# A transformer of four layers: where the second bias of the feed-forward part is added

## The reference

```
mod = silu(c) @ w_ada + b_ada                    # 6 rows of 288 per sample: shift, scale, gate, twice
x = x + gate_1 * (attention(norm(x) modulated) @ wo + bo)
h = gelu((norm(x) modulated) @ w1 + b1)          # 1152 hidden channels
x = x + gate_2 * (h @ w2 + b2)
```

## Time and profile before

| | before |
|---|---|
| median of three runs | 2198.0 us (2194.46 to 2200.98) |
| profiled execution | 2202.24 us, span 2200.5 us |
| PE busy | 2004.8 us (91%), mean granted clock 0.946 |
| DVE busy | 1336.7 us (61%) |
| ACT busy | 1142.4 us (52%) |
| POOL busy | 208.3 us (9%), 311 instructions |

### The profile page before, as it was taken

The page is one execution under the profiler, slowest core; times in us unless marked ns, Lnnn a source line. Parts: engine busy times, 40 slices in busy tenths (PEclk is TensorE's granted clock), DMA queues, the critical chain, the costliest instruction groups (busy, mean ns, idle before and its releaser), DMA issues.

```text
span 2200.5 us, 38987 instructions
## 1 busy us (share of the span) xinstructions
PE 2004.8 (91%) x15592; PEld 1496.7 (68%) x15592; DVE 1336.7 (61%) x2940; ACT 1142.4 (52%) x1705; POOL 208.3 (9%) x311
## 2 busy tenths in 40 slices
PE   6988999899998999999899999989997898999998
PEld 4346578748974896698575566887886646474658
DVE  4747647656674677476658482463545858684842
ACT  2353734474656365545636556554344474747463
POOL 3000111111110110011110000001100000000001
PEclk9686999899989999999999999998899999999999
DMA  5234242343234232524331412446154141314101
GB/s 160 60 120 85 74 122 63 73 122 92 77 68 136 64 86 48 152 67 100 78 104 18 131 7 65 68 78 134 30 107 111 31 114 36 96 20 112 26 3 25
DMA packets 204731, 173.97 MB, mean 79 GB/s; under 512 B 54822, under 2 KB 164678, under 8 KB 204550
## 3 DMA queue, kind: packets, MB, share of 16 engines
q1 hardware_dynamic: 197974, 158.76, 31.0%
q0 software_dynamic: 6576, 12.71, 2.1%
HBM read 125.57 MB, written 40.11 MB: 75 GB/s over the span
## 4 chain that ended last, share of the span: by engine, by line
PE 61%; DVE 20%; ACT 11%; DMA 3%; issue 3%; SPq 2%; POOL 0%; ACTq 0%; POOLq 0%; DVEq 0%
PE PSA L1890 16%; PE PSA L1905 14%; DVE MX L1529 9%; PE PSA L1680 5%; PE PSA L1794 4%; PE PSA L1771 4%; PE PSA L1741 4%; ACT PB L1378 4%; PE PSA L1784 3%; PE PSA L1753 2%; DVE HH L1659 1%; PE PSA L1814 1%; PE PSA L1703 1%; DVE FL L1429 1%; ACT FH L1408 1%
## 5 line engine op out<-in xcount | busy, mean ns | idle before, releaser
L1529 DVE TENSOR_REDUCE MX<-PSA 128x1 f32<-128x512 f32 x768 | 490.2, 682 | 292.9 <-PE PSA L1771 289.8
L1890 PE MATMUL PSA<-A,FH 128*128 128x256 f32 x2520 | 442.1, 290 | 14.0 <-DVE HH L1659 9.9
L1905 PE MATMUL PSA<-FH,HH 128*128 128x288 f32 x2016 | 443.2, 311 | 3.9 <-DVE HH L1659 3.3
L1415 ACT ACTIVATE HH<-PSA 128x512 fp32r<-128x512 f32 x252 | 150.6, 598 | 561.5 <-PE PSA L1890 552.0
L1378 ACT ACTIVATE PB<-PSA 128x1024 f32<-128x1024 f32 x384 | 370.8, 1026 | 86.4 <-PE PSA L1784 85.8
L1890 PEld LDWEIGHTS PSA<-A,FH 128*128 128x128 f32 x2520 | 362.3, 194 | 37.4 <-issue 18.7
L1905 PEld LDWEIGHTS PSA<-FH,HH 128*128 128x128 f32 x2016 | 327.1, 193 | 41.0 <-issue 32.6
L1905 PE MATMUL PSA<-FL,HH 128*128 128x288 f32 x1008 | 301.7, 299 | 0.0
L1771 PE MATMUL PSA<-KS,QS 54*128 54x512 f32 x768 | 221.4, 504 | 29.8 <-DVE MX L1529 12.2
L1283 POOL TENSOR_TENSOR X<-X,TM 128x288 f32<-128x288 f32 x128 | 101.3, 809 | 1455.2 <-DVE TM L1594 1455.2
L1659 DVE TENSOR_TENSOR HH<-PSA,HH 128x512 fp32r<-128x512 f32 x252 | 172.1, 683 | 85.1 <-ACT PSA L1416 84.5
(11 more groups left out here) (171 smaller groups left out, 2258.8 us busy)
## 6 DMA issues: line engine op xcount, KB each, us to landing
qkd<-HH SPq DMA_DIRECT2D x48, 504.0 KB
ST<-in_L_cond_w SPq DMA_DIRECT2D x51, 432.0 KB
ST<-in_L_cond_w SPq DMA_DIRECT2D x102, 192.0 KB
QS<-qkd SPq DMA_DIRECT2D x88, 144.0 KB
KS<-qkd SPq DMA_DIRECT2D x88, 144.0 KB
QS<-qkd SPq DMA_DIRECT2D x144, 72.0 KB
KS<-qkd SPq DMA_DIRECT2D x144, 72.0 KB
ST<-in_L_cond_w SPq DMA_DIRECT2D x153, 48.0 KB
```

What stands on the lines that cost most here:

```text
L1415: e.activation(r(HH[u][:, 0, :]), PS[bk][:, :], gelu)
L1529: e.reduce_max(MX[p // 2 % 2][:, col:col + 1], PS[bk][:, :], axis=AX.X).then_inc(free[bk], 1)
L1890: m = e.matmul(PS[bk][:, s_ * 256:(s_ + 1) * 256], r(w_), r(x_[:, half * 256:(half + 1) * 256]), start=(z == 0), stop=(z == 6))
L1905: m = e.matmul(PS[bk][:, 0:C], r(HH[u][:, c, tk]), r(w_), start=False, stop=(j == NCH - 1 and z == 2))
```

## The change

For items 4 to 15 (layers 1 to 3) the product of L1903 is gone; the first of the `fc2` products opens the sum instead. `B2` is made only in layer 0. `B2S` becomes a tile of 128 partitions, filled with `b2` of the layer by a DMA from POOL's queue, once per item. After each `gates` step for the feed-forward gate of items 4 to 15 stands a new step `bias`: POOL waits for the row of `b2`, for the gate row and for the item's second norm, multiplies both rows into `B2S`, adds `B2S` to the item's four tiles of `X`, and issues the DMA for the next item. The next `gates` DMA on SP's queue waits for that multiplication.

```diff
@@ prep_f
-        if n_ % NCH == 0:
+        if n_ % NCH == 0 and PIECES[k][0] == 0:
             put("b2", n_ // NCH, b2_free.get(n_ // NCH % 2))
             yield
+        elif n_ == 4 * NE * NCH:
+            put("b2row")
+            yield
@@ gates
-        put("gates", i, g, gr_ready[i // 4, g], gb_free[g])
+        put("gates", i, g, gr_ready[i // 4, g], gb_free[g], n_bias[0] if g else 0)
         gb_ready[g] += 16
+        if g and i >= 4:
+            put("bias", i, gb_ready[1], 4 * (norm_of[i] + 1))
+            n_bias[0] += 1
@@ build
-        B2S = sb("B2S", [2, C])
+        B2S = sb("B2S", [128, C])
@@ sp_program, gates
                     w.wait_ge(free[gr[0]], gr[1] + 1)
+                    w.wait_ge(s_bias, biased)
@@ pool_program
+                elif kind == "b2row":
+                    w.wait_ge(s_ramp, ramp)
+                    e.dma_start(B2S[:, :], layers[1]["b2"][0].to_broadcast([128, C])).then_inc(s_b2i, 16)
+                elif kind == "bias":
+                    i, gb, normed = a
+                    b = i % 4
+                    w.wait_ge(s_b2i, 16 * (4 * NE + i - 3))
+                    w.wait_ge(s_gb[1], gb)
+                    w.wait_ge(s_xn, normed)
+                    e.tensor_tensor(B2S[:, :], GB[:, 1, :], B2S[:, :], ALU.mult).then_inc(s_bias, 1)
+                    w.wait_ge(s_bias, i - 3)
+                    for q in range(QT):
+                        e.tensor_tensor(X[:, b * QT + q, :], X[:, b * QT + q, :], B2S[:, :], ALU.add).then_inc(s_ramp, 1)
+                        ramp += 1
+                    if i + 1 < NI:
+                        w.wait_ge(s_ramp, ramp)
+                        e.dma_start(B2S[:, :], layers[(i + 1) // 4]["b2"][0].to_broadcast([128, C])).then_inc(s_b2i, 16)
                 elif kind == "res":
+                    w.wait_ge(s_ramp, ramp)
@@ pe_program, fc2
                     if j == 0:
+                        may_fill(bk, n)
+                    if j == 0 and i < 4:
                         w.wait_ge(s_init, 18)
                         w.wait_ge(s_b2, n_ // NCH + 1)
-                        may_fill(bk, n)
                         e.matmul(PS[bk][:, 0:C], r(ON[:, :]), r(B2[(n_ // NCH) % 2][:, :]), start=True, stop=False)
                     for z, (c, w_) in enumerate(((0, wh), (1, wh), (0, wl))):
-                        m = e.matmul(PS[bk][:, 0:C], r(HH[u][:, c, tk]), r(w_), start=False,
+                        m = e.matmul(PS[bk][:, 0:C], r(HH[u][:, c, tk]), r(w_), start=(i >= 4 and j == 0 and z == 0),
```

More of the change, by code:

```diff
@@ L586, in at2_steps @@
         yield
-    gb_ready, gb_free = [0, 0], [None, None]
+    gb_ready, gb_free, n_bias = [0, 0], [None, None], [0]
     def gates(i, g):
-        put("gates", i, g, gr_ready[i // 4, g], gb_free[g])
+        put("gates", i, g, gr_ready[i // 4, g], gb_free[g], n_bias[0] if g else 0)
         gb_ready[g] += 16
+        if g and i >= 4:
+            put("bias", i, gb_ready[1], 4 * (norm_of[i] + 1))
+            n_bias[0] += 1
     def residual(i, q, bk, g, e_=None):
@@ L693, in fc2 @@
                     w_free["F", j] = done
-                    if j == NCH - 1:
+                    if j == NCH - 1 and L == 0:
                         b2_free[(n_ // NCH) % 2] = done
@@ L969, in build @@
         s_gelu = sem("hidden_written")
+        s_bias = sem("bias_gated")
         s_fc2 = sem("fc2_tile_done")
@@ L1207, in sp_program @@
                 elif kind == "gates":
-                    i, g, gr, old = a
+                    i, g, gr, old, biased = a
                     w.wait_ge(free[gr[0]], gr[1] + 1)
+                    w.wait_ge(s_bias, biased)
                     if old is not None:
@@ L1263, in pool_program @@
                     L, e_, _ = PIECES[k]
-                    e.dma_start(B2S[:, :], layers[L]["b2"][e_].to_broadcast([2, C])).then_inc(s_b2i, 16)
+                    e.dma_start(B2S[0:2, :], layers[L]["b2"][e_].to_broadcast([2, C])).then_inc(s_b2i, 16)
                 elif kind == "b2":
@@ L1271, in pool_program @@
                         w.wait_ge(*old)
-                    e.tensor_copy(r(B2[u][0:2, :]), B2S[:, :]).then_inc(s_ramp, 1)
+                    e.tensor_copy(r(B2[u][0:2, :]), B2S[0:2, :]).then_inc(s_ramp, 1)
                     ramp += 1
                     w.wait_ge(s_ramp, ramp)
-                    e.tensor_tensor(r(B2[u][0:2, :]), B2S[:, :], B2[u][0:2, :], ALU.subtract).then_inc(s_ramp, 1)
+                    e.tensor_tensor(r(B2[u][0:2, :]), B2S[0:2, :], B2[u][0:2, :], ALU.subtract).then_inc(s_ramp, 1)
                     ramp += 1
```

## The result

The kernel after takes 2212.81 us in the median of five runs (2207.92 to 2214.22). Beside 2198.0 us that is 14.8 us more: a ratio of 1.0066, 95% interval [1.0049, 1.0083]. A second series gave 1.0056 [1.0036, 1.0077]. The forecast was 2202 us with 2210 as its upper end: the side was right, the size was not.

What follows compares the result with a forecast made beforehand. TensorE was taken to carry 61% of the chain, DVE 20%, ScalarE 11%, POOL nothing. Products -3.3, meetings +5.9 and DMAs +1.5 us gave +4.1 on 2198.0, so 2202 us, range 2192 to 2210 us.

Steps and rivals of the forecast that it cites:

- The removed products: TensorE, items 4 to 15: 48 products gone, 18 of them on the chain; gain 3.3 us, ends 2.5 and 6.7.
- Who meets POOL: DVE's SBUF instructions beside POOL's additions, windows of items 5, 6, 11, 12: cost 5.9 us, ends 0 and 9.8.
- The discount for work off the chain: Item 11's window: only about half of DVE's work is on the chain, so meetings there cost 0.6 us.
- rival 2: Shared port decides: five DVE meetings in each of four windows, 9.8 us; total +8.8 us, 2207 us; chance 0.15.
- the rule of the Trainium skill's page: DVE and POOL's shared SBUF ports: a meeting could cost POOL's whole 0.79 us, 7.9 us in three windows; set aside.
- POOL's queue: Item 8: bias step delays layer 3's modulation loads some 8 us, hidden with about 4 us left; 1.0 us taken.
- rival 3: Late loads of layer 3's modulation make TensorE wait: 4 us, +7 us with the rest, 2205 us; chance 0.08.
- DMAs: Row DMA per item beside other transfers: 0.5 us at item 7, 1.0 at item 8; cost 1.5 us, ends 0 and 4.
- The sum: All terms together: -3.3 + 5.9 + 1.5 = +4.1 us, 2202 us; chance 0.55 together with the no-change rival.

Runs made afterwards that it cites:

- five2: Kernel before with four more bias products ahead of each of the 48 (192 more): 2211.4 us, 1.0057 of before.
- no_bias: The change with no second bias for items 4 to 15: no products, no POOL step, no row DMA; 2200.92 and 2195.83 us, 0.9994 and 0.9992 of before.
- both: The change with TensorE's 48 products left where they were, beside POOL's work: 2212.69 us, 1.0049 of before.
- timed_both: The kernel timed with TensorE's 48 products kept: 2200.16 us, 1.0004 of before.
- timed: The change, POOL's bias step waiting for a TensorE product (layers 1, 3) or put behind attention (layer 2): 2206.25, 2208.08, 2204.01 us; 1.0026, 1.0034, 1.0032 of before.
- memsets: The change with POOL's five operations per item replaced by 14 memsets of B2S, bias left out of items 4 to 15: 2207.36 us, 1.0039 of before.
- vt_first: The change with item 10's bias step alone moved behind the attention of item 11, so behind the VT memset: 2209.14 us, 1.0041 of before.
- no_dma: The change with the b2 row loaded once instead of twelve times, so other values are added: 2206.06 us, 1.0034 of before.
- dma_only: The change without POOL's five operations per item, keeping its waits and the row's DMA, bias left out: 2196.31 us, 1.0008 of before.

## Why the prediction was wrong

**The removed products: right, as far as it shows.** Forty-eight products are worth 3.1 us by five2, which added them, against 3.3 forecast; counting the pieces on the chain at the pitch of one, and a fifth of the rest, held. That their removal gave this back is not shown: no_bias is 1 to 2 us (4.4 at an equal clock) below before, both 1.2 above the change, timed_both below timed.

**Who meets POOL: right in kind and place, too small.** I foresaw meetings in the windows of items 5, 6, 11 and 12, and there they were, shown by memsets and timed, which take them away. The term was 5.9 us; the stages grew by 8.4. Items 5 (1.7 forecast, 1.8) and 12 (1.9, 2.1) were near; item 6 has 2.2 for 1.7 (1.7 stretched in the second profile). The miss is item 11: I took 0.6 us since only about half of DVE's work is on the chain there, and the stage grew by 2.3, of 2.6 stretched (1.7 us if all profiles with meetings there are set against all profiles without). The discount for work off the chain was wrong; that the delay is passed on through DVE's in-order queue is my reading of it. And a meeting costs the tiny instructions 0.56 us (0.16 to 0.72), not 0.47. My figure came from the earlier trace rows, where POOL had been adding for 0.19 us when NB (1167.63) came: it waited only for the rest. In a row of meetings each waits for a whole operation. This is rival 2, whose 9.8 us of meetings in these four windows was nearer than my 5.9; I gave it 0.15. Its total of 2207 us was too low all the same, as it lacks the memset too.

I had set aside the rule of the Trainium skill's page "SBUF — State Buffer" (section "SBUF: two separate sides"), a lock for the whole instruction, because the rows showed under 0.5 us a time. The trace agrees with the rule: the ends of DVE's tiny instructions fall on those of POOL's. Its price in my text, 7.9 us for the windows of items 5, 6 and 12, was an upper end: they grew by 6.1 us, where I had summed 5.3. What I had taken for a shorter lock was a lock met after it had begun. The same sentence says that two SBUF inputs are held up only against a GpSimd operation that reads SBUF; memsets shows that too, with no two-input instruction longer.

**POOL's queue: the step that failed.** "POOL's queue is in order, and the `bias` step stands ahead of the loads for layer 3's modulation": I asked that question for item 8 alone, and of DMAs alone. The memset of `VT` stands behind item 10's bias in the same queue, and I didn't ask who waits for it: the sum put it at nothing without a reason. It is worth 3.5 us (4.4 less 0.9 in the stage of item 10; with vt_first 0.7 are left of them), by stages that scatter by 1 to 2 us. For item 8 I was right that it is hidden: the load is issued at 1511.10 and becomes the chain's piece for 8.50 us, as rival 3 has it, but TensorE starts on it 22.4 us behind the gate DMA's issue (1497.27 to 1519.64), where it was 23.4 before: it took the place of the wait for the read-back, at the same price. Rival 3's wait came, its 4 us didn't (the stage of item 8 is at -2.3 in the change and -3.5 without the step, the one that scatters most).

**DMAs: not settled.** I had 1.5 us. The change is 2 us (equal clock) to 6 us (runs) over no_dma. The stage of item 10 has 2.7 us of it: no_dma's memset starts 2 us less behind the gate DMA's issue, 1 us by the DMA that isn't issued ahead of it and 1 us by a gate row that landed sooner. So this part belongs to the memset. Alone the DMAs cost nothing (dma_only). That their price hangs on the arithmetic beside them was not in my text.

**The sum, again:** -3.1 for the products, +8.4 meetings, +3.5 memset, which is +8.8; with the 1.7 us of the remaining stages, where the DMAs' price would be, it is +10.5, and 11.8 us was measured in the mean of all runs. The median of the first five lies 14.8 us up, above that by scatter. That it fell outside my range is therefore partly chance; the mean, 2210.8, lies just beyond the upper end as well. About 5 us of the 11.8 go with a lower granted clock (0.9465 in the mean over the change's runs, 0.9498 before), and 7.0 are left at an equal one. Whether the pauses of TensorE that the meetings and the memset make bring the lower clock, no experiment here settles: no_bias, which has neither, ran at 0.9460 and 0.9487 in its two series, and the first `TM` of layer 0, ahead of all that was changed, starts anywhere from 144.6 to 158.6 us in the twenty profiles.

## What to carry to other kernels

When work goes to an idle in-order engine, walk down that engine's queue behind *every* place where it is put, and ask for each instruction there, memsets included, who waits for it: waiting cost next to nothing here, and the 4 us of work behind the wait did cost. Small VectorE instructions with two inputs in SBUF each take about as long as one GpSimd instruction that reads SBUF when the two meet, and nearly all of it was passed on here, even where half of the work was off the chain. A later place in the list doesn't move work in a queue that is otherwise empty; a wait does. And before shifting work off a busy engine, price it by adding more of it: four times the products showed that there were about 3 us to win (1.9 to 4.3).

## What the runs showed of the hardware

- Fourteen memsets by GpSimd (5.84 us) beside VectorE's two-input instructions stretch none of them, where each operation of 0.77 us that reads SBUF holds one of them up. Of ten 128x512 copies with one input, four took 0.52 to 0.63 us beside the memsets in place of 0.42.
- GpSimd is held up in turn by the 512-wide copy and subtraction: four additions take 3.58 to 3.72 us beside them (items 5, 11, 12), 3.06 beside the tiny ones alone (item 6) and 3.03 beside none (item 10).
- Two DMAs issued 0.3 us apart: the read-back of 576 KB took 8.33 us in place of 4.29 (one trace). With the 147 KB one 1.5 to 1.8 us ahead it took 4.20 to 5.08 (ten traces).
- Twelve runs of one kernel spread over 11 to 27 us, and go with the mean granted clock by 1.5 us for each 0.001 of it. With twelve runs of a kernel, 3 us were hardly to be seen in the time, but they were in stages of the trace.
